# Two transformer layers on one core: the two batches staggered at the three borders between attention, feed-forward and the next layer

## The reference

```
x = x + gate_a * attention(scale_a * norm(x) + shift_a)
x = x + gate_f * ffn(scale_f * norm(x) + shift_f)
```

## Time and profile before

| | |
|---|---|
| time, median of 3 runs | 695.38 us (692.64 to 696.22) |
| the profiled execution | 692.95 us |
| its span, first to last instruction | 691.2 us |
| its mean granted TensorE clock | 0.985 |
| busy: TensorE, VectorE, ScalarE, GpSimd | 92%, 56%, 43%, 21% |

### The profile page before, as it was taken

The page is one execution under the profiler, slowest core; times in us unless marked ns, Lnnn a source line. Parts: engine busy times, 40 slices in busy tenths (PEclk is TensorE's granted clock), DMA queues, the critical chain, the costliest instruction groups (busy, mean ns, idle before and its releaser), DMA issues.

```text
span 691.2 us, 11404 instructions
## 1 busy us (share of the span) xinstructions
PE 632.5 (92%) x4051; PEld 513.5 (74%) x4059; DVE 389.3 (56%) x730; ACT 294.2 (43%) x435; POOL 144.7 (21%) x143
## 2 busy tenths in 40 slices
PE   4998888999899999999999897789999999999995
PEld 3777666867688888888888675456558788888884
DVE  6477424777544445544456869992348713335445
ACT  3557355333433333333332553527770544333331
POOL 5511024504422222222221000000213042222220
PEclk9999999999999999999999999999999999999999
DMA  8445367310111111111100030413321001111101
GB/s 320 112 177 181 105 177 187 88 42 1 46 47 46 46 46 46 46 46 46 46 23 1 1 125 0 127 56 95 87 86 47 1 24 46 46 46 46 46 23 61
DMA packets 27200, 48.94 MB, mean 71 GB/s; under 512 B 4672, under 2 KB 9184, under 8 KB 27168
## 3 DMA queue, kind: packets, MB, share of 16 engines
q1 hardware_dynamic: 26848, 48.38, 23.0%
q10 hardware_dynamic: 320, 0.13, 0.1%
HBM read 36.57 MB, written 11.93 MB: 70 GB/s over the span
## 4 chain that ended last, share of the span: by engine, by line
PE 70%; DVE 14%; issue 4%; ACT 4%; SPq 3%; DMA 3%; POOL 1%; DVEq 1%; ACTq 0%
PE PS L494 34%; PE PS L867 16%; DVE nmx L1335 4%; PE PS L753 3%; PE PS L725 3%; PE PS L767 3%; SPq L320 2%; PE PS L632 2%; PE PS L630 2%; DMA qk_slot<-k_scr 2%; DVE x L1409 1%; DVE xn L1405 1%; DMA w_raw<-in_wqkv 1%; POOL qk_lo L464 1%; DVE stats L1243 1%
## 5 line engine op out<-in xcount | busy, mean ns | idle before, releaser
L1116 ACT ACTIVATE qk_hi<-xn 128x512 fp32r<-128x512 f32 x82 | 51.8, 632 | 177.2 <-DVE xn L1517 138.8
L494 PE MATMUL PS<-h_hi,wqkv_hi 128*128 128x512 f32 x352 | 122.4, 407 | 4.1 <-POOL wqkv_hi L458 2.1
L494 PE MATMUL PS<-h_hi,wqkv_lo 128*128 128x512 f32 x336 | 114.0, 397 | 0.0
L1514 DVE TENSOR_TENSOR pr<-pr,PS 128x512 f32<-128x512 f32 x60 | 41.2, 687 | 86.8 <-PE PS L494 86.8
L494 PEld LDWEIGHTS PS<-h_hi,wqkv_hi 128*128 128x128 f32 x352 | 68.3, 194 | 19.3 <-POOL wqkv_hi L458 2.3
L1519 DVE TENSOR_TENSOR qk_lo<-xn,qk_hi 128x512 fp32r<-128x512 f32 x74 | 51.3, 693 | 52.7 <-ACT qk_hi L1116 52.7
L494 PE MATMUL PS<-h_lo,wqkv_hi 128*128 128x512 f32 x184 | 74.3, 404 | 0.0
L494 PEld LDWEIGHTS PS<-h_hi,wqkv_lo 128*128 128x128 f32 x336 | 63.6, 189 | 13.4 <-issue 0.2
L1112 ACT ACTIVATE pr<-PS 128x512 f32<-128x512 f32 x82 | 48.8, 596 | 42.8 <-PE PS L494 42.6
L867 PE MATMUL PS<-wqkv_hi,qk_hi 128*128 128x256 f32 x336 | 62.1, 284 | 3.4 <-POOL qk_lo L464 1.7
L458 POOL TENSOR_TENSOR wqkv_hi<-fw_raw,wqkv_hi 128x768 fp32r<-128x768 f32 x21 | 41.4, 1969 | 113.3 <-ACT wqkv_hi L1105 113.3
(11 more groups left out here) (214 smaller groups left out, 1232.1 us busy)
## 6 DMA issues: line engine op xcount, KB each, us to landing
fw_raw<-in_ffn SPq DMA_DIRECT2D x41, 384.0 KB, 3.0
qk_slot<-q_scr SPq DMA_DIRECT2D x64, 132.0 KB
q_scr<-qk_hi SPq DMA_DIRECT2D x16, 256.0 KB
q_scr<-qk_lo SPq DMA_DIRECT2D x16, 256.0 KB
qk_slot<-k_scr SPq DMA_DIRECT2D x64, 64.0 KB
wmod<-in_wmod SPq DMA_DIRECT2D x1, 1536.0 KB, 13.1
x<-in_x SPq DMA_DIRECT2D x2, 512.0 KB, 4.0
wmod<-in_wmod SPq DMA_DIRECT2D x1, 1024.0 KB, 9.6
```

Source lines behind the costliest of these rows:

```text
L494: ins = nc.tensor.matmul(dst, left(a, c), right(b, c), start=n == 0, stop=n == total - 1)
L1116: nc.scalar.activation(hidR[b][0], hid[b], ACT.Copy).then_inc(f["hi"], 1)
L1514: tt(hid[b] if half is None else gu[b], gact[b], PS[:, 5, :], ALU.mult).then_inc(f["gu"], 1)
```

## The change

Every border lets batch 0 go ahead of batch 1.

1. **Attention into feed-forward (both layers).** The output projection of batch 0 moves into `values_pass`: tiles 0 and 1 in the iteration g=5, tiles 2 and 3 in g=6. VectorE does batch 0's gate, addition, statistics and norm between `outputs(4)` and `outputs(6)`, TensorE its transposes ahead of the last `values`. `out_projection` holds only batch 1. The 30 fillers go. ScalarE, no longer VectorE, modulates batch 0.
2. **Start of the feed-forward.** EARLY becomes 3. The first three units are tiles 0 to 2 of batch 0, the next three the same tiles of batch 1; buffers go by u % 2. Batch 1's norm, its transposes, the router's logits and the zeroing of the accumulators stand between the early units. Tiles 2 and 3 (and 24) get weight buffers of their own (`fwE`).
3. **End of the feed-forward.** The last TAIL = 3 tiles of layer 0 (2 of layer 1) are done for batch 0 first and then for batch 1. Batch 0's gate, addition and statistics stand on VectorE ahead of the unit k=4 of six (k=3 of four), its norm ahead of the last unit.
4. **Between the layers.** `shifts1` moves into feed-forward 0, behind `down(6)`. `gates(1)` moves into `maxima_pass(1)` in the place of 9 fillers, `gate_steps(1)` to VectorE's end of that pass. 8 fillers and batch 0's transposes stand ahead of the last `down`. `project1` of batch 0 has batch 1's transposes in its middle, and batch 1's projections start one unit of scores later.
5. PSUM banks are handed out anew; in layer 1 the values have one bank (6) in place of two, so quad g's `values` wait for the transposition of quad g-1.

```diff
-EARLY = 2
+TAIL = [3, 2]
+EARLY = 3
-O_BANK = [6, 7]
+O_BANK = [[6, 7], [6, 6]]
+        def weights(i, s):
+            if isinstance(i, int) and (2 <= i < 4 or i == TILES[0] - 1):
+                return fwE[i % 2]
+            return fwR[s]
+        def tail(l):
+            n, first = TAIL[l], TILES[l] - TAIL[l]
+            return [(2 * first + k, k // n, first + k % n) for k in range(2 * n)]
...
 # TensorE, values_pass
                     keys_major(l, SLOTS * g + 2)
+                    if g == BQ + 2:
+                        if l:
+                            pe.wait_ge(y_gated, 4 * B + 1)
+                        project_out(l, 0, range(OC), True, (2, 3))
                     values(l, g - 1, (1,))
                     keys_major(l, SLOTS * g + 3)
+                    if g == BQ + 1:
+                        pe.wait_ge(split, (1, 3)[l])
+                        pe.wait_ge(at[l]["ol"], BQ)
+                        project_out(l, 0, range(OC), True, (0, 1))
                     values(l, g - 1, (2, 3))
+                norm_transposes(2 * l + 1, (0,))
                 values(l, QUADS - 1, range(NT))
...
 # TensorE, out_projection
-                filler(30, 7)
 # TensorE, ffn
+                pe.wait_ge(hl_ready, 4 * n + 2)
+                early_up(0)
+                early_up(1)
+                pe.wait_ge(h_ready[0], 2 * n + 2)
+                zero(0, 1)
+                early_down(0)
+                early_up(2, (0,))
+                norm_transposes(n, (1,))
+                early_up(2, (1,))
+                early_down(1)
+                logits(l)
+                zero(2, 3)
+                early_down(2)
+                pe.wait_ge(hl_ready, 4 * n + 4)
+                early_up(3)
+                early_up(4)
+                early_down(3)
+                early_up(5)
                 combine_rows(l)
+                early_down(4)
                 combine_table(l, 0)
+                up(EU, 0, w3, EARLY)
+                early_down(5)
                 if HALVES[l] > 1:
                     combine_table(l, 1)
+                up(EU + 1, 1, w3, EARLY)
+                down(EU, 0, w3)
+                if l == 0:
+                    pe.wait_ge(cB_ready, HALVES[0] * B)
+                    shifts1()
+                pair(2, w3)
+                with pe.Fori(3, LOOPS[l]) as p:
                     pair(p)
+                for u, b, i in units:
+                    up(u, b, weights(i, i % 2), i)
+                    down(*previous)
+                    previous = (u, b, weights(i, i % 2))
+                if l == 0:
+                    pe.wait_ge(shifts1_taken, 1)
+                    filler(8, 7)
+                    norm_transposes(2, (0,))
+                down(*previous)
...
 # TensorE, between the layers
-            shifts1()
-            gates(1)
-            filler(7, 4)
-            norm_transposes(2)
             for m in range(4):
                 project1(0, m)
-            maxima_pass(1, ([[lambda m=m: project1(1, m)] for m in range(4)], [[]] * SLOTS))
+                if m == 2:
+                    norm_transposes(2, (1,))
+            maxima_pass(1, ([[]] + [next1(*ms) for ms in ((0,), (1,), (2, 3))], [[]] * SLOTS))
...
 # ScalarE, end of ffn
+                units = tail(l)
+                for u, b, i in units[:-1]:
+                    unit(u, u % 2, True)
+                    if u - units[0][0] < TAIL[l] - 1:
+                        weights_high(l, (i + 1) // 2, (i + 1) % 2)
+                u = units[-1][0]
+                unit_silu(u, u % 2)
+                if l == 0:
+                    normalise(2, 0)
+                unit_high(u, u % 2, True)
+                if l == 0:
+                    modulate(2, 0)
+                    h_high(2, 0)
...
 # VectorE
+            def attention_outputs(l):
+                n = 2 * l + 1
+                for g in range(BQ):
+                    outputs(l, g)
+                dve.wait_ge(y_ps, 4 * l + 1)
+                aggregate = gate_and_add(l, 0, 0, 0, Y0_BANK[l][0])
+                outputs(l, BQ)
+                aggregate()
+                dve.wait_ge(y_ps, 4 * l + 2)
+                aggregate = gate_and_add(l, 0, 0, 1, Y0_BANK[l][1])
+                aggregate()
+                norm_scales(n, slice(0, 1))
+                outputs(l, BQ + 1)
+                normalise(n)
+                outputs(l, BQ + 2)
+                outputs(l, BQ + 3)
+                h_low(n, 0)
+                gate_and_add_batch(l, 0, 1, (Y1_BANK, Y1_BANK + 1), y_ps, (4 * l + 3, 4 * l + 4))
+                early_product(l, 0)
+                norm_scales(n, slice(1, B))
+                early_product(l, 1)
+                early_product(l, 2)
+                h_low(n, 1)
...
 # VectorE, router0
-                early_product(0, 0)
-                chosen = ranks(masked[:, :, :], 4, E, tri, lambda i: early_product(0, i + 1) if i < EU - 1 else None)
+                early_product(0, 3)
+                chosen = ranks(masked[:, :, :], 4, E, tri, lambda i: early_product(0, 4) if i == 2 else None)
                 then(tt(masked[:, :, :], prob[:, :, :], chosen, ALU.mult))
                 combine_parts(masked[:, :, :], E)
+                early_product(0, 5)
...
 # VectorE, end of ffn
+                for k, (u, b, i) in enumerate(units):
+                    if k == TAIL[l] + 1:
+                        out_of_ffn(0)
+                    if l == 0 and k == len(units) - 1:
+                        norm_scales(2, slice(0, 1))
+                    unit(u, u % 2, b, (i - SHT[l]) % HALVES[l])
+                if l == 0:
+                    h_low(2, 0)
+                out_of_ffn(1)
+                if l == 0:
+                    norm_scales(2, slice(1, B))
```

More of the change, by code:

```diff
@@ L541, in gates, with norm_transposes @@
                 ins.then_inc(mod_ps, 1)
-            def norm_transposes(n):
-                for b in range(B):
+            def norm_transposes(n, batches=range(B)):
+                for b in batches:
                     pe.wait_ge(xn_ready[b], n + 1)
@@ L946, in _ @@
             out_projection(1)
-            norm_transposes(3)
-            zero(0, 1, 2, 3)
-            logits(1)
             ffn(1)
@@ L1151, in ffn @@
-                pair(0, early_unit, True)
-                pairs = TILES[l] // 2
-                pair(1, unit, True, beside=(take_rows, take_table))
-                for start, end in SPANS[l]:
-                    with act.Fori(start, end - (end == pairs)) as p:
-                        pair(p, unit, True, start)
-                pair(pairs - 1, unit, TILES[l] % 2)
-                if TILES[l] % 2:
-                    for b in range(B):
-                        unit(4 * pairs + b, b, True)
-            for i in range(2):
-                weights_high(0, 0, i)
@@ new lines, in pair @@
+                            if b == 0 and (s == 0 or following):
+                                weights_high(l, p + s, 1 - s)
+                early_silu(0)
+                weights_high(l, 1, 0)
+                early_high(0)
+                early_silu(1)
+                normalise(n)
+                early_high(1)
+                early_silu(2)
+                modulate(n, 1)
+                h_high(n, 1)
+                early_high(2)
+                weights_high(l, 1, 1)
+                router(l)
@@ new lines, in ffn @@
+                for start, end in SPANS[l]:
+                    with act.Fori(start, end) as p:
+                        pair(p, True, start)
+                units = tail(l)
+                for u, b, i in units[:-1]:
[6 more added lines that the diff above has]
+                    normalise(2, 0)
@@ L1372, in maxima_rest @@
                         maxima(l, g, s)
-            def outputs_pass(l):
-                for g in range(QUADS):
-                    outputs(l, g)
             for m in range(4):
@@ L1416, in add_output_bias, with gate_and_add_batch @@
+            def gate_and_add_batch(l, which, b, banks, done, counts):
+                first = None
+                for i in range(2):
+                    dve.wait_ge(done, counts[i])
+                    last = gate_and_add(l, which, b, i, banks[i])
+                    if first:
+                        first()
+                    first = last
+                if first:
+                    first()
             def add_output_bias():
                 dve.wait_ge(loaded["bo"], 16)
-                gated_bias = ytmp[:, 0:B, :]
+                gated_bias = ytmp[0][:, 0:B, :]
@@ L1501, in router1 @@
                 combine_parts(masked[:, :, 0:E], E)
-                for u in range(1, EU):
+                for u in range(4, EU):
                     early_product(1, u)
@@ L1525, in pair @@
                         for b in range(B):
-                            if half is not None and isinstance(p, int) and b == 0:
-                                dve.wait_ge(cB_ready, sum(HALVES[:l + 1]) * B)
-                            unit(4 * p + 2 * s + b, b, half)
-                pair(1, 1)
```

(13 more changed lines are left out.)

392 lines of the change are left out of this document (198 added, 194 removed).

## The result

The changed kernel takes 717.95 us (713.5 to 722.17, four runs) where the kernel before takes 694.29 on the same chip: 3.4% longer, ratio 1.034 with a 95% interval of 1.030 to 1.038. The direction was as forecast. The size was not: I named 706, at most 714. The profiled execution took 716.13, its span is 714.4 and its mean granted clock 0.955, where before it was 692.95, 691.2 and 0.985.

A forecast was written before the change was run, and what follows sets the result against it. TensorE was taken to bound the feed-forwards, VectorE the borders and layer 1's maxima pass. Terms 1.5 + 5.3 + 8.3 + 0.3 - 6.2 + 3.5 = +12.7 on 692.95 gave 705.6, named 706; range 694 to 714.

The forecast's parts named there:

- the clock's part: Half-rate loss inside the forecast terms: 1.7 behind `shifts1` and 1.9 after the 6.3 wait for batch 1's norm-2 transposes.
- border 1: Attention 0 to up(8): feed-forward starts 10.8 earlier, given back as moved work and waits on VectorE's router; +1.5, bounds -3 to +4.
- border 3: Attention 1 to up(8): feed-forward 1 starts near 532 instead of 544.36, router short; -6.2, bounds -9 and -4.
- `shifts1`: In feed-forward 0, no longer covered: 3.63 on TensorE plus 1.7 of half clock behind; +5.3, bounds 3.6 and 5.5.
- up(44) to the maxima pass: Feed-forward 0's tail to layer 1's full pass: two weight waits of 3.4, late batch 1 norm, half clock; +8.3, bounds +4, +11.
- +0.3: Gates in the maxima pass: 16 matmuls in the place of 9 fillers, mostly covered by VectorE; up to +2 at half clock.
- product 4's wait: Layer 0's up(5) waits 4.5 because product 4 stands behind four long steps of `ranks` on VectorE.
- the combining transposes: Between up(5) and up(7) of layer 0: a further wait of 2.5 after product 4's.
- Tail of feed-forward 1: up(28) to the last addition: one weight wait of 3.4, last `down` 1.0 late; +3.5, bounds +3 and +4.5.
- Table loads: Rival: three more ScalarE loads delay silu on the path, 3 x 1.28 = 3.8, giving 710; chance 0.06. Forecast counted none.
- The tail's weights are in time: Rival: up(45), up(46) and up(29) don't wait (10.2 in all), giving 695.5, no change; chance 0.07.
- TensorE stays fed: Rival: VectorE-ScalarE-GpSimd delivers all five handovers in time, so removed fillers and idle time come back; -26, 669; chance 0.13.

The follow-up runs named there:

- e2: Changed kernel with dense fillers laid into TensorE's seven long waits, nothing else touched: 702.96 us, ratio 1.012 to the kernel before.
- e1: Kernel before, without its fillers ahead of the norm transposes (30 at each attention's end, 7 between the layers): 698.32 us, ratio 1.0063.
- e5: Changed kernel with VectorE's product 4 of feed-forward 0 behind the first long step of the ranks instead of the fourth: 715.56 us, ratio 1.033.
- e4: Changed kernel with `shifts1` moved from the middle of feed-forward 0 into the first weight wait of its tail: 709.5 us, ratio 1.024.
- e10: e9 plus a one-element silu right behind the router's exponential (sigmoid in layer 1), to load the table in idle time: 686.11 us, ratio 0.988.
- e3: Changed kernel with own buffers for tile 23 (15 in feed-forward 1) and tail weight copies issued one unit earlier: 701.71 us, ratio 1.010.
- e9: e7 with one dense filler ahead of each of the eight pairs of shifts: 687.4 us, ratio 0.990.
- e7: e6 with `shifts1` replacing the fillers at up(5), and batch 0's fourth projection ahead of batch 1's norm-2 transposes: 689.7 us, ratio 0.9944.
- e6: Changed kernel with e3's early tail weights and e2's fillers in the four waits left: 690.67 us, ratio 0.9955.

## Why the prediction was right and wrong

**Right: the sign, the places and the waits.** Without the clock's part the forecast sum is +9.1, and e2 measured +9.9, of which 1.6 or more is still clock. Single terms were off by 1 to 2 each and partly cancel. The staggering at border 1 gains nothing (+1.5 forecast: the shifts, which stand where up(8) would, start 3.4 after the up(8) of before, and 0.2 after it in e2), it gains at border 3 (-6.2 forecast, -4.9 measured), and batch 1's late norm makes the stretch between the layers longer.

**Wrong: the clock, at 3.6 instead of 13.3 or more.** The step that failed is the clock's part of three terms. I wrote "half of about 3.4 is lost, 1.7" behind `shifts1` and "I expect the same after 6.3, +1.9" ahead of the scores, and charged nothing at the waits of 3.4, 3.4, 4.5, 2.2 and 3.4 that stood in the same forecast. I had tied the fall to the longest idle time because the one at hand was 8.94; here it came with waits of 3.0 to 4.4 as well. By e2 the clock took at least 4.8 up to up(9) (counted 1.7), 5.6 to the maxima pass's end (counted 1.9) and 2.9 at the end (counted none). By e1 the removed fillers themselves had a worth of 4 to 5, and I had priced their removal at nothing. The Trainium skill ("TensorE: Matmul & The Clock Gate", section "What's actually happening") calls the half clock the default that activity releases. The trace agrees at the six waits of the changed kernel (0.51 to 0.56 in their windows above, 1.00 again after 3.4 to 13.7 us), and I applied it at one of these waits alone. At e5's wait of 3.43 the clock stayed at 1.00, so the fall is likely there, not certain.

**`shifts1`: +5.3, measured 6.4** (e4): 4.8 for the 32 matmuls, which took 3.63 where they were covered, and 1.7 for the clock. The 1.7 is as forecast; what was missing is that the clock can fall while the shifts still run (from 202.4, in e2 only behind them), and so the upper bound of 5.5 was too low.

**up(44) to the maxima pass: +8.3 and +0.3, measured 11.0.** The two weight waits came as forecast (3.79 and 3.43 for 3.4 each). The wait for batch 1's norm was 4.41 instead of 6.3, since the third projection (1.88) runs ahead of it too. At least 5.6 were the clock's.

**Border 1: two waits that were one.** I listed product 4's wait (4.5), then the combining transposes (2.5 more). e5 shows one wait, the router's: take away the first and the second takes all of it.

**Tail of feed-forward 1: +3.5, measured 6.9.** The weight wait is the forecast one (3.43); 2.9 of the rest are the clock's.

**Table loads.** ScalarE loads nine tables instead of six, the three more that I counted. I called them covered; but one in each layer makes up(4) wait 0.74, and in layer 0 the load stands in the chain of waits. They weren't covered, since the load stands behind ScalarE's wait and not in it. That rival's mechanism exists. Its size of 3.8 is not borne out (0.74 twice on TensorE), but e10 couldn't measure what it is. The 2.66 for a switch, by which the prediction's estimate went, is not seen: the load takes 1.28, and the next activation starts right behind it (167.00 to 168.29).

**The other rivals.** "The tail's weights are in time" would have given 695.5 against the forecast's 706, that is 10.2. e3 made it true, and it was worth 16. "TensorE stays fed" needed the waits 16 shorter than forecast and would have given 669; no run comes near that, not even e9 (687.4) with waits removed and filled.

**Is the staggering itself of use?** With its weight waits gone, its shifts in a wait and the clock held, it beats the kernel before by about 1% (e9, 687.4 against 695.6 beside it). In e7's profile the gain is -4.4 between the layers and -4.9 at border 3, and nothing at border 1; its clock is 0.990 where the profile before has 0.985, so a part of these gains is the clock's. What the kernel before would gain from the same care for its clock was not tried, so how much of the 1% is the staggering's stays open.

## What to carry to other kernels

A filler that only keeps the clock up is part of the kernel: before removing one, or opening a wait on TensorE, price some of the dense work behind it at the half rate. Do so for every wait like those here (2.0 to 4.4 us), not only for the longest, and for narrow matmuls as well. Two waits in a row behind one slow chain are one wait; an experiment that shortens the first shows it at once. Splitting a loop's last tiles by batch takes away the cover of the weights' preparation, so prepare those tiles one unit earlier before judging the split.

## What the runs showed of the hardware

- In the changed kernel the granted clock fell to the 1.2 GHz level at all six idle times of TensorE of 3.0 to 4.4 us, between 1.9 us after their start and 0.9 after their end. Over all twelve profiles, without the wait for the first transfer, it fell in the wait or within about 1 us of its end at 20 of the 21 waits of 3.0 to 7.9 us (not at e5's 3.43) and at 10 of the 12 of 2.0 to 2.7 (not at the 2.13 and 2.21 of the kernel before). Filled with dense matmuls (e2) five of the six places kept 1.00; at the sixth it fell 4 us later, behind narrow matmuls.
- It also fell with TensorE busy all the time: in or behind 32 matmuls of 2 columns in nine of ten profiles (e4: 0.65, e7: 0.55; not e6) and, in some executions, behind 32 of 16 columns (e10: 0.51 from 161 to 168). With one 512-column matmul ahead of every four of the narrow ones it stayed at 1.00 (e9, e10).
- Executions of one kernel differ in their mean granted clock. The twelve of e7 go from 683.7 at 0.990 to 692.1 at 0.980; the six of e9, all at 0.990 to 0.992, lie within 1.9.
- TensorE's three waits for GpSimd of 3.4 to 3.8 cost about 5 each (e3: 10.6 of waits, 15.5 of time).
- ScalarE's table load took 1.28 each time in both kernels, and an activation that was ready started right behind it.
